# Attention scores from whole float32 q and k in 32-row products, three score banks, and a ring of two PSUM banks

## The reference

```python
x = x + tanh(g_xattn[0]) * L0_xattn(layernorm(x), ctx)     # 16 heads of 8, rotary q and k, 77 keys
x = x + tanh(g_ffn[0])   * L0_ffn(layernorm(x))            # softmax router, 1 of 8 experts, relu
x = x + tanh(g_xattn[1]) * L1_xattn(layernorm(x), ctx, ctx, mask)
x = x + tanh(g_ffn[1])   * L1_ffn(layernorm(x))            # 2 of 8 experts, silu
# attention: scores = q @ k.T / sqrt(8) per head, softmax over the keys, @ v, @ Wo
```

## Time and profile before

| | |
|---|---|
| runs | 452.20, 454.81, 459.82 us (median 454.81) |
| profiled execution, first to last instruction | 464.2 us |
| TensorE busy with products | 314.7 us, 68% |
| VectorE busy | 264.1 us, 57% |
| ScalarE busy | 136.3 us, 29% |
| GpSimd busy | 152.2 us, 33% |
| mean granted TensorE clock | 0.828 |

### The profile page before, as it was taken

The page is one execution under the profiler, slowest core; times in us unless marked ns, Lnnn a source line. Parts: engine busy times, 40 slices in busy tenths (PEclk is TensorE's granted clock), DMA queues, the critical chain, the costliest instruction groups (busy, mean ns, idle before and its releaser), DMA issues.

```text
span 464.2 us, 7008 instructions
## 1 busy us (share of the span) xinstructions
PE 314.7 (68%) x1932; PEld 228.1 (49%) x1932; DVE 264.1 (57%) x916; ACT 136.3 (29%) x302; POOL 152.2 (33%) x172
## 2 busy tenths in 40 slices
PE   2468999989754095751467999999530298888920
PEld 2236555545353094640256566654320297777820
DVE  2768668773675244353367667765545066665634
ACT  2412354535313033220103454354200033333300
POOL 3211212051423134561102102165766134555550
PEclk9767799999985579795567999999855599999985
DMA  7434032100000867823231313000103677988708
GB/s 268 126 74 118 12 80 52 43 11 19 17 8 29 224 215 215 243 73 90 62 85 36 71 27 85 14 24 23 42 29 100 213 244 236 299 249 289 235 12 269
DMA packets 39997, 52.93 MB, mean 114 GB/s; under 512 B 7177, under 2 KB 24334, under 8 KB 39968
## 3 DMA queue, kind: packets, MB, share of 16 engines
q1 hardware_dynamic: 33648, 45.03, 33.7%
q0 software_dynamic: 3584, 6.36, 3.9%
q10 hardware_dynamic: 2736, 1.20, 0.9%
HBM read 35.58 MB, written 9.64 MB: 97 GB/s over the span
## 4 chain that ended last, share of the span: by engine, by line
PE 21%; DVE 8%; issue 7%; DMA 6%; SPq 4%; POOL 4%; ACT 1%; POOLq 0%; DVEq 0%; ACTq 0%
POOL routed L445 3%; PE ps_s L750 2%; PE ps_a L730 2%; DMA xt<-routed 2%; PE ps_a L731 2%; PE ps_s L821 2%; SPq L342 2%; PE ps_s L751 2%; PE ps_t L705 2%; PE ps_n L765 2%; PE ps_a L838 1%; PE ps_d L765 1%; PE ps_t L821 1%; DMA probs<-expert_out 1%; DMA routed<-pay,slot 1%
## 5 line engine op out<-in xcount | busy, mean ns | idle before, releaser
L463 POOL DMA_INDIRECT expert_out<-yo,rows_at x64 | 63.0, 984 | 81.5 <-DVE yo L1179 63.6
L529 ACT ACTIVATE probs<-ps_s 103x512 f32<-103x512 f32 (+1 forms) x96 | 56.3, 597 | 56.8 <-PE ps_s L751 53.3
L445 POOL DMA_INDIRECT routed<-pay,slot x48 | 48.4, 1009 | 58.3 <-DVE slot L1132 47.8
L1025 DVE TENSOR_REDUCE negm<-ps_a 128x4 f32<-128x308 f32 x128 | 55.1, 470 | 19.5 <-PE ps_a L731 18.0
L750 PE MATMUL ps_s<-qs,ks 128*103 128x512 f32 (+1 forms) x96 | 46.2, 481 | 2.0 <-ACT augT L522 1.2
L731 PE MATMUL ps_a<-ks,qs 128*128 128x308 f32 x128 | 43.1, 374 | 5.9 <-DVE negm L1025 5.6
L421 POOL TENSOR_SCALAR ve<-mv 128x4 f32<-128x4 f32 x16 | 4.0, 251 | 116.0 <-DVE mv L975 116.0
L751 PE MATMUL ps_s<-augT,aug 128*103 128x512 f32 (+1 forms) x96 | 39.6, 412 | 0.0
L838 PE MATMUL ps_a<-cst,xt 128*128 128x128 f32 x32 | 11.1, 355 | 39.8 <-DMA xt<-routed 38.2
L731 PEld LDWEIGHTS ps_a<-ks,qs 128*128 128x128 f32 x128 | 28.9, 227 | 15.4 <-DVE negm L1025 6.6
L821 PE MATMUL ps_s<-xT,probs 128*128 128x128 f32 x208 | 32.5, 299 | 2.9 <-DVE xT L1190 1.7
(11 more groups left out here) (168 smaller groups left out, 659.3 us busy)
## 6 DMA issues: line engine op xcount, KB each, us to landing
probs<-f_in SPq DMA_DIRECT2D x40, 384.0 KB
qs<-qhl SPq DMA_DIRECT2D x128, 64.0 KB, 2.0
probs<-f_in SPq DMA_DIRECT2D x24, 321.0 KB
xt<-routed SPq DMA_DIRECT2D x32, 65.0 KB
probs<-routed SPq DMA_DIRECT2D x32, 65.0 KB
yin<-expert_out SPq DMA_DIRECT2D x8, 256.0 KB, 4.4
routed<-pad ACTq DMA_DIRECT2D x18, 65.0 KB
x<-x_in SPq DMA_DIRECT2D x4, 256.0 KB, 7.6
```

What stands on the lines that cost most here:

```text
L445: pool.indirect_dma_start(out=routed[l], out_offset=bass.IndirectOffsetOnAxis(ap=slot[c][:, t:t + 1], axis=0), in_=pay[c][:, t, :], in_off ...
L463: pool.indirect_dma_start(out=expert_out[l], out_offset=bass.IndirectOffsetOnAxis(ap=rows_at[i % SHORT][:, :], axis=0), in_=yo[i % SHORT][ ...
L529: nc.scalar.activation(probs[n % 2][0:KSIZE[j], s, :], ps_s[(NS * n + s) % SCORE_BANKS][0:KSIZE[j], :], ACT.Exp, scale=SCALE).then_inc(exp ...
L1025: nc.vector.tensor_reduce(negm[:, i, g * HPG:(g + 1) * HPG], a[:, 0:GK].rearrange("p (h k) -> p h k", h=HPG), AX.X, ALU.max, negate=True). ...
```

## The change

`SCORE_BANKS` becomes 3 and `RING` becomes 2. q and k stay whole float32. `qT` is q in its 128 channels, and group g's 32 channels are its partitions 32g to 32g+31. `ks[l]` holds the block-diagonal keys in the same partitions, one for each layer. A product of group g contracts over those 32 rows only. `high_q`, `low_q`, `spread_q`, `spread_keys`, `take_keys` and the `select` matrix are gone. Score tiles are issued three at a time (`TOGETHER`), their groups all different: first three 32-row products, then the three products with `aug`. The units for the maximum now go through the groups before the tokens, and all units of a step (one or two) are issued together in the same way.

```diff
-SCORE_BANKS, RING = 2, 3
+SCORE_BANKS, RING, TOGETHER = 3, 2, 3
+ROWS = P // GROUPS
...
-KEYS_SPREAD_AT = [-18, LAST + 24]
-BLOCKS_AT = [-17, LAST + 27]
+BLOCKS_AT = [-20, LAST + 13]
...
-        khl = [sb(f"khl{i}", [P, NB * KEYS], F32R) for i in range(2)]
-        ks = sb("ks", [P, GROUPS, NB, GK], F32R)
-        qhl = [sb(f"qhl{i}", [P, SEQ], F32R) for i in range(2)]
-        qs = [sb(f"qs{i}", [P, GROUPS, SEQ], F32R) for i in range(3)]
+        ks = [sb(f"ks{l}", [P, NB, GK]) for l in range(LAYERS)]
+        qT = [sb(f"qT{i}", [P, SEQ]) for i in range(3)]
...
             def add_q(n):
                 pool.wait_ge(rot_ok, n + 1)
-                if n:
-                    pool.wait_ge(ql_ok, n)
-                nc.gpsimd.tensor_tensor(qr1[:, :], qr1[:, :], qr2[:, :], ALU.add).then_inc(q_ok, 1)
+                if n >= 3:
+                    pool.wait_ge(sc_full, NS * (n - 2))
+                nc.gpsimd.tensor_tensor(qT[n % 3][:, :], qr1[:, :], qr2[:, :], ALU.add).then_inc(q_ok, 1)
...
-            def scores_for_max(n, u):
+            def scores_for_max(n, units):
...
+                banks = {}
+                for u in units:
+                    i, g = divmod(u, GROUPS)
+                    banks[u] = ring()
+                    if l:
+                        if n == NB and u == 0:
+                            pe.wait_ge(maskT_ok, 1)
+                        nc.tensor.matmul(banks[u][:, 0:GK], maskT[:, i * P:(i + 1) * P], aug[:, g, :], start=True, stop=False)
+                for u in units:
+                    i, g = divmod(u, GROUPS)
+                    rows = slice(ROWS * g, ROWS * (g + 1))
+                    nc.tensor.matmul(banks[u][:, 0:GK], qT[n % 3][rows, i * P:(i + 1) * P], ks[l][rows, b, :], start=not l, stop=True).then_inc(ring_full, 1)
...
-            def scores(n, s):
+            def scores(n, first):
...
+                for s in range(first, first + TOGETHER):
+                    j, g = score_tile(s)
+                    k = NS * n + s
+                    if k >= SCORE_BANKS:
+                        pe.wait_ge(exp_ok, k - SCORE_BANKS + 1)
+                    rows = slice(ROWS * g, ROWS * (g + 1))
+                    nc.tensor.matmul(ps_s[k % SCORE_BANKS][0:KSIZE[j], :], ks[l][rows, b, KROWS * j:KROWS * j + KSIZE[j]], qT[n % 3][rows, :], start=True, stop=False)
+                for s in range(first, first + TOGETHER):
+                    j, g = score_tile(s)
+                    k = NS * n + s
+                    nc.tensor.matmul(ps_s[k % SCORE_BANKS][0:KSIZE[j], :], aug[:, g, KROWS * j:KROWS * j + KSIZE[j]], augT[n % 2][:, :], start=False, stop=True).then_inc(sc_full, 1)
...
-                    if 0 <= k < NB * NS:
+                    if 0 <= k < NB * NS and k % TOGETHER == 0:
                         scores(n0 + k // NS, k % NS)
-                    for b, u in max_units(k):
-                        scores_for_max(n0 + b, u)
+                    for b in range(NB):
+                        scores_for_max(n0 + b, [u for c, u in max_units(k) if c == b])
```

More of the change, by code:

```diff
@@ L330, in _ @@
             sp.dma_start(pad[:, :], pad_in).then_inc(ld_pad, 16)
[L332 to L342, removed]
+            sp.dma_start(w[1][:, :], w_in[1]).then_inc(ld_w[1], 16)
             def load_tiles(l):
@@ L389, in _ @@
             for l in range(LAYERS):
[L390 to L393, removed]
                 load_tiles(l)
@@ L509, in copy_nT @@
                 nc.scalar.activation(nT[:, :], ps_t[:, :], ACT.Copy).then_inc(nT_ok, 1)
[L511 to L515, removed]
-                nc.scalar.activation(qhl[0][:, :], qr1[:, :], ACT.Copy).then_inc(qh_ok, 1)
             def copy_augT(n):
@@ L630, in _ @@
                         copy_nT(n0 + b)
-                    for b in due("high", k):
-                        high_q(n0 + b)
-                        if n0 + b == 0:
-                            act.wait_ge(ld_aug, 16)
-                            nc.scalar.activation(aug[:, :, :].rearrange("p g k -> p (g k)"), augf, ACT.Copy).then_inc(s_aug, 1)
+                    if l == 0 and k == SET_UP_AT:
+                        act.wait_ge(ld_aug, 16)
+                        nc.scalar.activation(aug[:, :, :].rearrange("p g k -> p (g k)"), augf, ACT.Copy).then_inc(s_aug, 1)
                     for b in due("augment", k):
@@ L671, in keys @@
                     nc.tensor.matmul(ring()[:, 0:NB * KEYS], w[l][:, c:c + D], cxk[:, :], start=True, stop=True).then_inc(ring_full, 1)
-            def spread_keys(l):
-                pe.wait_ge(k_split, l + 1)
-                if l:
-                    pe.wait_ge(exp_ok, NS * NB * l)
-                else:
-                    pe.wait_ge(s_select, 3)
-                for g in range(GROUPS):
-                    if g >= 2:
-                        pe.wait_ge((k_even, k_odd)[g % 2], 2 * l + 1)
-                    bank = ps_s[g % 2][:, 0:NB * KEYS]
-                    for c in range(2):
-                        last = nc.tensor.matmul(bank, select[:, c, g, :, :].rearrange("p c r -> p (c r)"), khl[c][:, :], start=c == 0, stop=c == 1)
-                    last.then_inc(k_full, 1)
             def values(l, j):
@@ L716, in front @@
                 transposes(lambda i: nrm[:, i, :], nrmT_ok, nT_ok, n + 1)
-            def scores_for_max(n, u):
+            def scores_for_max(n, units):
                 l, b = divmod(n, NB)
-                g, i = divmod(u, TPB)
-                if u == 0 and b == 0:
+                if b == 0 and units and units[0] == 0:
                     pe.wait_ge(ks_ok, 2 * (l + 1))
-                if i == 0:
-                    pe.wait_ge(qspread[n % 3][g], 64 * (n // 3 + 1))
-                bank = ring()
-                if l:
-                    if n == NB and u == 0:
-                        pe.wait_ge(maskT_ok, 1)
-                    nc.tensor.matmul(bank[:, 0:GK], maskT[:, i * P:(i + 1) * P], aug[:, g, :], start=True, stop=False)
-                nc.tensor.matmul(bank[:, 0:GK], qs[n % 3][:, g, i * P:(i + 1) * P], ks[:, g, b, :], start=not l, stop=True).then_inc(ring_full, 1)
+                if units and units[0] == 0:
+                    pe.wait_ge(q_ok, n + 1)
+                banks = {}
[10 more added lines that the diff above has]
+                    nc.tensor.matmul(banks[u][:, 0:GK], qT[n % 3][rows, i * P:(i + 1) * P], ks[l][rows, b, :], start=not l, stop=True).then_inc(ring_full, 1)
             def augmenting(n):
@@ L1225, in _ @@
                         rotate(n0 + b)
-                    for b in due("low", k):
-                        low_q(n0 + b)
                     for b in due("output", k):
```

83 lines of the change are left out of this document (17 added, 66 removed).

## The result

| | before | after |
|---|---|---|
| median of the runs | 454.81 us (448.78 to 459.82, 5 runs) | 622.61 us (619.66 to 637.62, 5 runs) |
| profiled execution, span | 464.2 us | 635.8 us |
| mean granted TensorE clock | 0.828 | 0.696 (0.699 to 0.716 in the other runs) |
| TensorE busy with products | 314.7 us | 462.5 us |

The ratio is 1.373, with an interval of 1.3606 to 1.3854. The medians grew by 167.8 us where 69.3 were forecast, and the time lies outside the stated ranges (500 to 550, and 476 to 568). The profiled execution is the longest of the five, 15 us above their median. The other four differ from it by 3 us to 18 us, so it serves for the shape and not for the last few microseconds.

A forecast was written before the change was run, and what follows sets the result against it. TensorE's start-to-start distances were taken to bound the blocks. Six blocks +61.2, last blocks +3.4, starts +1 and +5, tail -1.3 gave +69.3 us and a 524 us median; range 500 to 550, wider range 476 to 568 (0.8).

The forecast's parts named there:

- The step that failed: Blocks with scores beside units: TensorE bounds them at full clock, with work for 20.35 of 21.0 us in layer 1.
- triple: Three score tiles issued together in a block: 1.89 us instead of 1.56, +0.33 each, +1.3 a block.
- pair with masks: Two units for the maximum with their mask products in layer 1: 0.85 + 0.28 us at full clock.
- passes in program order: Rival for score and unit products: a product's second pass holds up the next product's first; 563 us, chance 0.10.
- no sharing: Rival for score and unit products: 32-row products do not share the array at all; 603 us, chance 0.07.
- price for a changed shape: Around score triples and unit groups: going in and out costs TensorE 0.24 us, the larger first weight load 0.07.
- Ring of two: Five places a block where TensorE waits for VectorE's read of a unit, some 0.5 us each: +2.6 us.
- ring and exponentials: In blocks with units: 2.6 us of bank waits plus 0.4 for a third score bank coming late.
- VectorE, ScalarE and the DMAs hidden in the blocks: Work removed from VectorE and ScalarE, and SyncE's 128 DMAs, was already hidden in these blocks: no time gained.
- Starts: Units of each layer's first block: layer 0 +1 us (-0.7 to +3.4), layer 1 +5 us (+2.6 to +8).

The follow-up runs named there:

- alone: Separate kernel, not the model: ten wait-free stretches of TensorE products of different heights, from rest; one or two float32 strips took 34.5 us at half clock.
- wide_f32r: Changed kernel with full-height products (zeros outside the group), q and k rounded once to F32R, no spreading; 512.15 us, ratio 1.1277.
- wide_r_lean: Changed kernel with full-height F32R products, old banks, tiles one by one, zeroing moved off GpSimd's path, keys built later; 456.03 us, ratio 1.0083.
- alone2: Separate kernel, not the model: ten more wait-free TensorE stretches, including zero-filled rows and mixes begun at full clock; 64 rows by ones took 34.5 us.
- wide_f32: Changed kernel with score and unit products both of 128 rows, keys zero outside the group, still float32; 584.33 us, ratio 1.2939.
- units_wide: Changed kernel with only the units for the maximum at full height (zeros outside the group), score tiles still 32 rows by threes; 567.3 us.
- scores_wide: Changed kernel with only the score tiles at full height, units still 32 rows by ones and twos; 625.22 us, ratio 1.3913.
- fill2: Changed kernel with two useless 128-row F32R products added ahead of each unit's product, except in the first block; 603.31 us.
- fill1: Changed kernel with one useless 128-row F32R product added ahead of each unit's product, except in the first block; 631.59 us.
- ring3_quick: Changed kernel with two score banks, a ring of three, tiles by twos, and the maximum reading only 8 of 77 keys; 552.41 us.
- ring3: Changed kernel with the old banks, two for scores and a ring of three, and score tiles by twos; 598.64 us.
- before_ring2: Kernel before with three score banks and a ring of two, nothing else; 472.24 us, ratio 1.0511.

## Why the prediction was wrong

**The step that failed** stands in the first paragraph: "both at the full clock of 2.4 GHz", taken over from the earlier trace rows for a block whose products would no longer be the same. Every term of the sum was in microseconds at full clock. The blocks had 0.57 to 0.86 of it. The six grew by 144.1 us instead of 61.2. That is 83 of the 102 us by which the growth of the span (635.8 - 464.2 = 171.6) exceeds the forecast's 69.3. The other 27.5 us of the growth, where the forecast had 8.1, are 12.2 ahead of the first block's exponentials and 15.3 between the last block of layer 0 and the first of layer 1 (below). From the start of the last block on, both executions take 155.0 us. No rival was about the clock either.

**Products.** Right at full clock: triple 1.83 for 1.89 us, pair with masks 1.10 for 1.13. The rival "passes in program order" and the rival "no sharing" are refuted: six passes in 1.04 us in the change, and by twos the time of by ones in `alone`. The price for a changed shape, read off `weigh`, held for strips of rows too. A part of it is no price of the shape: before, the step of 0.31 or 0.32 us instead of 0.24 also follows the 128 x 128 transposes (67.39 to 67.71 us).

**Ring of two.** The places were right. All five wait where the prediction put it: the output projection (0.66 us) and the pair behind it (0.70) in the lines above, the pair behind the projection of q (0.70, at 405.62), and these two, the single and the router product:

```profile
416.48 0.62 PE L668 MATMUL ps_a<-aug,maskT 128*128 128x308 f32 x1 [0.63 <-DVE negm L949]
433.94 1.85 PE L736 MATMUL ps_a<-w,nT 128*128 128x8 f32 x8 [0.66 <-DVE negm L949]
```

Together they are 3.35 us; the forecast had 2.6, at 0.5 each. In `wide_f32r`, whose two blocks above run at full clock with the ring, the groups and the three banks of the change, TensorE is without work for 4.65 and 4.13 us, 3.4 and 3.5 more than in the earlier trace rows. The forecast had 2.6 + 0.4 = 3.0 for ring and exponentials: a little low.

**VectorE, ScalarE and the DMAs hidden in the blocks.** Right: VectorE waits 183 us for the units' products, and in `wide_r_lean`, where all of this is gone and the products cost as before, the middle blocks take 20.4 and 21.1 us, as in the earlier trace rows.

**Starts.** Here the prediction did look at the clock (0.61 and 0.65 in the earlier trace rows), and took a value between full and half. It was half (0.50 from 27.3 to 50.2 us and from 316.7 to 340.3). The scores of layer 0 start 12.2 us later (first exponential at 53.2 instead of 41.0; forecast +1). The reads of its units begin 2.3 us sooner (28.7 instead of 31.0; forecast 4), but last 18.9 us instead of 7.2, and what stands between them and the first exponential takes 2.8 us longer. That is more than the forecast's 14.2 for half clock, because a read was left out of that term. It counted 1.77 us for a pair, with one read in it, but `scores_for_max` claims both banks before its first product, so both reads must be over. A pair takes 34.15 - 31.74 = 2.41 us, 1.01 of it waiting:

```profile
31.74 1.40 PE L672 MATMUL ps_a<-ks,qT 32*128 32x308 f32 x4 [1.01 <-DVE negm L949]
34.15 1.40 PE L672 MATMUL ps_a<-ks,qT 32*128 32x308 f32 x4 [1.01 <-DVE negm L949]
```

The sixteen units of layer 1 take 23.6 us (316.7 to 340.3, clock 0.50) against the 20.8 priced for half clock. What starting sooner gains is small: `wide_r_lean` shows 3.9 us sooner turned into 1.6.

**The clock, as far as it is shown.** The height of the products that work at a time is what decided here whether TensorE came back to 2.4 GHz: shown alone (`alone`, `alone2`), in the kernel (`wide_f32`, `units_wide`, `scores_wide`) and by adding work (`fill2`, though not `fill1`). The Trainium skill ("TensorE: Matmul & The Clock Gate", HAM oscillation) ties the lower clock to idle gaps between products. The stretches of ones and twos have no gap and stay at half, so that rule alone would have given the forecast's blocks too. Waits seem to matter on top: `ring3_quick` is 70 us below the change by its median, though its spread of 43 us leaves the size open.

**Open.** Which wait or which mix starts a fall; how the loss splits between waits and strips (the two act together, and no single edit separates them); why `fill1` and `ring3` differ so much from run to run; and why the ring of two alone costs 22.9 us in the medians while its blocks and its start account for 11.7. Part of that gap lies in the trace of before that it is read against: from the start of the last block on it takes 155.0 us, where `before_ring2` takes 148.5.

## What to carry to other kernels

A price per product holds at the clock at which it was read; if an edit changes the shape of most products, the clock of the stretch is a term of its own, and its bound is a factor of two. Packing small products into strips of rows paid here where three strips were filled and the products between kept TensorE at full clock (`units_wide` against `wide_f32`); for one or two strips, zeros that fill the rows were cheaper. If several products claim banks before the first of them is issued, all the reads of those banks stand in the wait. Before a change of this kind, run the new mix by itself, from rest: `alone` shows what no row of the old kernel could.

## What the runs showed of the hardware

- One or two strips of 32 rows, or 64 rows one at a time, back to back with no gap: granted clock 0.50 for 34.5 us (F32R strips: 26.0 us). Three strips, two of 64 rows, 96 rows and 128 rows: up to 1.00 within 6.5 us.
- The kernel's mixes of strips and full-height products kept 1.00 where they began with it and never waited (27.5 and 28.3 us); from rest they came to it after 27.1 us (triples) and not in 42.9 us (pairs).
- Products in different strips share the array in both passes: 40 passes of 512 columns by ones take 34.5 us, 80 by twos 34.5 at the same half clock, and 160 by fours 19.0 at mostly full clock.
- More products can take less time: `fill2` took 603.31 us and the change 622.61, with 224 products added.
